# Routing stage of a mixture-of-experts kernel: low parts of weights on VectorE, token products on ScalarE, zero tiles and expert 0's weights issued later

## Chip, cores and metric

The kernel runs on one core of a Trainium2 chip. The time is that of the device for one launch, in microseconds (us). TensorE multiplies matrices into PSUM, VectorE and ScalarE work on tiles of 128 partitions in SBUF and PSUM, GpSimd does the same from SBUF and issues the gathers, and SyncE issues all other transfers. Each engine runs its own instructions in order and meets the others at semaphores.

## The reference

Sixteen sequences of attention, then a feed-forward layer with 8 experts (two chosen for each row) and one shared expert, and a residual:

```python
x = x + ffn(cond(x, mask, Wq, Wo))            # x: (16, 256, 512), so 4096 rows of 512
# ffn(x):
logits = einsum("bsh,eh->bse", x, gate_w)      # 8 experts
probs = softmax(logits); top_w, top_i = top_k(probs, 2)
top_w = top_w / sum(top_w)                     # combine: top_w at the chosen experts, else 0
h = silu(x @ w_gate[e]) * (x @ w_up[e])        # width 352, for each expert e
moe = sum over e of combine[e] * (h @ w_down[e])
shared = (silu(x @ sw_gate) * (x @ sw_up)) @ sw_down     # width 1408
return moe + shared * sigmoid(x @ shared_gate_w)
```

Everything is float32. The kernel reaches that precision with three products of rounded parts: a = hi(a) + lo(a), where hi is the value rounded to TensorE's fast format and lo is a - hi; a matmul is then hi*hi + hi*lo + lo*hi.

## The kernel before, in words

The kernel has three parts, one behind the other: `attention` (to about 735 us), `experts` (735 to about 1331 us) and `shared`. The change is in `experts` alone, and there in what comes ahead of the first expert tile: the routing stage, 735 to 837 us.

**What the routing stage computes.** It has two strands which share the engines.

- *Routing.* VectorE takes the maximum, the softmax and the two best experts of each row, in a chain of small operations each of which waits for the one before (`link`). TensorE ranks the rows by expert (`rank`, two matmuls), VectorE makes from the ranks the start of each expert's tiles (`bounds`) and the slot of each row. To invert that list, from slot to row number, there are 16 rounds of 4 blocks of rows: in a round VectorE compares (`hot_ones`: `token_at`, 128x328, is 1 where a column is the slot's column; `is_row`, 128x512, where a partition is the slot's row), GpSimd multiplies the row numbers into `token_at` (`times_token`, L798 to 802), and TensorE sums four products of the two (`place_tokens`, 4 small matmuls into `ps_id`). `token_at` and `is_row` have two buffers, so `hot_ones` of a round waits until the matmuls of the round two before are done. At the end VectorE copies the sum to `token_of`, and GpSimd gathers the rows of the first tile with it.
- *The shared expert's upward half, for the first 512 rows.* Its width of 1408 is cut into SI = 11 chunks of 128, which are the 11 steps t of TensorE's loop. A step has 12 matmuls for the gate half ("gate(t)") and 12 for the other ("up(t)"), each 128x128 by 128x512. SyncE loads a chunk's raw weights (`load_up`, 2 x 256 KB, two buffers), ScalarE makes the high part (`up_high`) and GpSimd the low part (`up_low`, L804 to 808, 128x1024), both with two buffers; ScalarE takes silu of the gate half, VectorE multiplies (`up_h`), and SyncE stores the product to `held`, to be used much later.

**The order on each engine** is written out by hand:

- TensorE, step t: wait for the chunk's low part (`a_wlo`) and silu(t-2); gate(t); the first two rounds of `place_tokens` of the step; wait for the product t-2; up(t); in step 1 `rank`; two more rounds. The rounds are in steps 6 to 9 (FIRST = 6, `rounds_after`), four each.
- ScalarE, step t: wait for gate(t), silu(t); then `up_high(t+2)`, which waits for the chunk's transfer and, as its output buffer is that of chunk t, for up(t). At the end of step 8 it makes the high parts of expert 0 (`split(0, 0)`).
- GpSimd: constants and the zero tile; `up_low(0)` to `up_low(6)`; then for t from 6 the products of two rounds, `up_low(t+1)`, the products of two more.
- VectorE: the routing chain, in which `up_h(0)` to `up_h(4)` are placed; then for t from 6 to 10 `hot_ones` of two rounds, `up_h(t-1)`, `hot_ones` of two more. After round 16 it makes `token_of`, the low parts of expert 0, the last product, and the low part of the first tile.
- SyncE's queue: the 512 rows, chunks 0 and 1, expert 0's weights (`load(0)`, 2.1 MB in four transfers), nine zero tiles into `routed` (512 KB each; slots without a row must read as zero); then in step t: wait for low part t, `load_up(t+2)`, wait for product t, store it. Behind the loop: expert 1's weights, and the wait for the zero tiles, before which no tile may be stored.

In the lists of rows a helper's line stands for all its uses: L1089 is a matmul of gate or up, L808 `up_low`, L801 `times_token`, L861 `up_high`, L872 silu, L946 `up_h`, L1025 and L1027 `hot_ones`, L1076 `place_tokens`, L739 `load_up`, L733 to L735 `load`, L748 the zero tiles, L846 and L911 the parts of an expert's weights. The buffers of the chunks' parts are those of expert 1: chunk 0, 2, ... stand as `e_hi_g` and `e_lo_g`, chunk 1, 3, ... as `e_hi_u` and `e_lo_u`; the matmuls of `place_tokens` write `e_ps_r`, and up(t) of odd steps `e_ps_y`.

Of the kernel before, what the change touches and what calls it, by code (L numbers as in the profile page):

```python
# [586 lines left out]
def experts(nc, ctx, sems, keep, attn, w_gate, w_up, w_down, sw_gate, sw_up, held, routed):  # L587
# [7 lines left out]
    P = 128  # L595
# [47 lines left out]
    RO = 4  # L643
# [74 lines left out]
        return ap.rearrange("p (a w) -> p a w", a=1).to_broadcast([P, RO, width])  # L718

    FIRST = 6  # L720

    def rounds_after(t, part):

# [5 lines left out]
    @block.sync  # L729
    def _(sp):  # L730
        def load(e):
            for k, w in enumerate((w_gate, w_up)):
                sp.dma_start(raw[k][:], w[bass.ds(e, 1), :, :].rearrange("e (k p) i -> p (e k) i", p=P)).then_inc(raw_in, 16)  # L733
            sp.dma_start(raw[2][:, 0:FULL, :], w_down[bass.ds(e, 1), 0:FULL * P, :].rearrange("e (k p) h -> p (e k) h", p=P)).then_inc(raw_in, 16)
            sp.dma_start(raw[2][0:I - FULL * P, FULL, :], w_down[bass.ds(e, 1), FULL * P:I, :].rearrange("e p h -> p (e h)")).then_inc(raw_in, 16)  # L735

        def load_up(t):
            for k, w in enumerate((sw_gate, sw_up)):
                sp.dma_start(a_raw[t % 2][:, k, :, :], w[:, t * P:(t + 1) * P].rearrange("(k p) i -> p k i", p=P)).then_inc(a_raw_in[t % 2], 16)  # L739

        sp.dma_start(a_rows[:], attn[0:GT, :].rearrange("(s p) h -> p s h", p=P)).then_inc(a_rows_in, 16)
        load_up(0)
        load_up(1)
        load(0)

        sp.wait_ge(consts, 8)
        for j in range(FEWEST, NTILES):
            sp.dma_start(routed[j * ST:(j + 1) * ST, :].rearrange("(s p) h -> p s h", p=P), zeros[:]).then_inc(filled, 16)  # L748
        for t in range(SI):
            if t + 2 < SI:  # L750

                sp.wait_ge(a_wlo, t + 1)
                load_up(t + 2)
            sp.wait_ge(a_h_done, t + 1)
            sp.dma_start(held[t * P:(t + 1) * P, :], a_h[t % 2][:]).then_inc(a_stored[t % 2], 16)
        sp.wait_ge(lo_done, NPARTS)
        load(1)
        sp.wait_ge(filled, 16 * (NTILES - FEWEST))
        sp.wait_ge(bounds_done, 1)

        def start(e, n, first):
            if exists(e + 2):

                sp.wait_ge(lo_done, NPARTS * (e + 2))
                load(e + 2)

        def tile(j, n):
            sp.wait_ge(y_done, SB * (j + 1) + SB)
            sp.dma_start(routed[bass.ds(j * ST, ST), :].rearrange("(s p) h -> p s h", p=P), y[:]).then_inc(stored, 16)

        each_expert(sp, start, tile)
        total = sp.value_load(keep["bounds"][0:1, NE:NE + 1], min_val=1, max_val=NTILES - 1)
        for n in range(2):
            sp.wait_ge(a_stored[n], 16 * ((SI - n + 1) // 2))
        keep["load_ahead"](sp)
        alone(sp, stored, 16 * total + 16, consts, 8)

    @block.gpsimd
    def _(pool):
        pool.memset(ident[:], 0.0).then_inc(base, 1)  # L780
        pool.memset(before[:], 0.0).then_inc(base, 1)
        pool.iota(iota_e[:], pattern=[[1, NE]], base=0, channel_multiplier=0, allow_small_or_imprecise_dtypes=True).then_inc(consts, 1)
        pool.wait_ge(base, 2)

        pool.affine_select(out=before[:], in_=before[:], compare_op=ALU.is_ge, fill=1.0, base=0,
                           pattern=[[-1, P]], channel_multiplier=1).then_inc(consts, 1)
        pool.memset(every[:], 1.0).then_inc(consts, 1)
        pool.affine_select(out=ident[:], in_=ident[:], compare_op=ALU.not_equal, fill=1.0, base=0,
                           pattern=[[-1, P]], channel_multiplier=1).then_inc(consts, 1)
        for tile in (iota_r, iota_c):  # L790
            pool.iota(tile[:], pattern=[[1, tile.shape[1]]], base=0, channel_multiplier=0,
                      allow_small_or_imprecise_dtypes=True).then_inc(consts, 1)
        pool.iota(token[:], pattern=[[0, TOPK], [P, NBLK]], base=0, channel_multiplier=1,
                  allow_small_or_imprecise_dtypes=True).then_inc(consts, 1)
        pool.memset(zeros[:], 0.0).then_inc(consts, 1)

        def times_token(m, n):

            pool.wait_ge(col_hot, m + 1)
            of = token[:].rearrange("p k b -> p (k b)")[:, RO * m:RO * (m + 1)]  # L800
            pool.tensor_tensor(token_at[n][:], token_at[n][:], each(of, NCOL), ALU.mult).then_inc(token_hot, 1)  # L801

        def up_low(t):
            pool.wait_ge(a_whi, t + 1)  # L804
            if t >= 2:

                pool.wait_ge(a_u_mm, t - 1)
            pool.tensor_tensor(a_lo[t % 2], a_raw[t % 2][:], a_hi[t % 2], ALU.subtract).then_inc(a_wlo, 1)  # L808

        for t in range(FIRST + 1):  # L810
            up_low(t)
        for t in range(FIRST, SI):
            for m in rounds_after(t, 0):
                times_token(m, m % 2)
            if t + 1 < SI:
                up_low(t + 1)
            for m in rounds_after(t, 1):
                times_token(m, m % 2)
        pool.wait_ge(bounds_done, 1)
        pool.wait_ge(ids_done, 1)  # L820

        def gather(j):
            pool.tensor_copy(now[:], token_of[:, bass.ds(j * SB, SB)]).then_inc(now_done, 1)
            alone(pool, now_done, j + 1, ids_done, 1)
            for s in range(SB):
                pool.indirect_dma_start(out=rows[:, s, :], out_offset=None, in_=attn,
                                        in_offset=bass.IndirectOffsetOnAxis(ap=now[:, s:s + 1], axis=0)).then_inc(rows_in, 16)

        gather(0)

        def tile(j, n):

            pool.wait_ge(rows_in, 16 * SB * (j + 1))
            pool.wait_ge(t_mm, 2 * (j + 1))
            gather(j + 1)

        each_expert(pool, lambda e, n, first: None, tile)
        total = pool.value_load(keep["bounds"][0:1, NE:NE + 1], min_val=1, max_val=NTILES - 1)
        pool.wait_ge(rows_in, 16 * SB * (total + 1))

    @block.scalar
    def _(act):
# [14 lines left out]
        def up_high(t):  # L857
# [2 lines left out]
                act.wait_ge(a_u_mm, t - 1)  # L860
            act.activation(a_hi[t % 2], a_raw[t % 2][:], ACT.Copy).then_inc(a_whi, 1)  # L861

        for m in range(HT):
            act.wait_ge(a_t_mm, m + 1)
            act.activation(a_x_hi[:, m, :], a_ps_t[m % 2], ACT.Copy).then_inc(a_xhi, 1)
        up_high(0)
        up_high(1)
        for t in range(SI):
            act.wait_ge(a_g_mm, t + 1)
            if t >= 2:  # L870
                act.wait_ge(a_h_done, t - 1)
            act.activation(a_silu[t % 2][:], a_ps_g[t % 2], ACT.Silu).then_inc(a_silu_done, 1)  # L872
            if t + 2 < SI:
                up_high(t + 2)
            if t == SI - 3:
                split(0, 0)

        act.sem_inc(y_done, SB)
# [28 lines left out]
    def _(dve):  # L907
# [28 lines left out]
        def up_x_low():  # L936
            for m in range(HT):
                dve.wait_ge(a_xhi, m + 1)
                dve.tensor_tensor(a_x_lo[:, m, :], a_ps_t[m % 2], a_x_hi[:, m, :], ALU.subtract).then_inc(a_xlo, 1)

        def up_h(t):
            dve.wait_ge(a_silu_done, t + 1)
            dve.wait_ge(a_u_mm, t + 1)
# [9 lines left out]
        link(dve.tensor_tensor(B["prob"][:], B["expd"][:], wide(R["inv"][:]), ALU.mult))  # L953

        up_x_low()
        src = "prob"
        for m, ind, one, k in (("m1", "i1", "one1", 0), ("m2", "i2", "one2", 1)):
            link(dve.reduce_max(R[m][:], B[src][:], AX.X))
# [6 lines left out]
            if k == 0:  # L965
                link(dve.tensor_scalar(B["cand"][:], B["one1"][:], -2.0, None, ALU.mult))
                link(dve.tensor_tensor(B["rest"][:], B["prob"][:], B["cand"][:], ALU.add))
                src = "rest"
                up_h(0)
        dve.tensor_tensor(B["both"][:], B["one1"][:], B["one2"][:], ALU.add).then_inc(both, 1)  # L970

        link(dve.tensor_tensor(R["ws"][:], R["m1"][:], R["m2"][:], ALU.add))
# [3 lines left out]
        link(dve.tensor_scalar(R["sgd"][:], R["sge"][:], 1.0, None, ALU.add))  # L976
        link(dve.reciprocal(keep["shared_gate"][:], R["sgd"][:]))

        up_h(1)
        dve.wait_ge(ranked, 2)  # L980
        dve.tensor_copy(B["rank"][:], ps_r[:, 0]).then_inc(copied, 1)
        dve.tensor_copy(B["count"][:], ps_r[:, 1]).then_inc(copied, 1)
# [3 lines left out]
        while d < NBLK:  # L986
            link(dve.tensor_copy(B[b][:, 0:d, :], B[a][:, 0:d, :]))
            link(dve.tensor_tensor(B[b][:, d:, :], B[a][:, d:, :], B[a][:, 0:NBLK - d, :], ALU.add))
            a, b, d = b, a, 2 * d
        up_h(2)  # L990
        link(dve.tensor_scalar(S["total"][:], B[a][:, NBLK - 1, :], 1.0 / ST, (ST - 1.0) / ST - 0.5 + 0.25 / ST, ALU.mult, ALU.add))
        link(dve.tensor_scalar(S["tiles"][:], S["total"][:], ROUND, -ROUND, ALU.add, ALU.add))
        link(dve.tensor_scalar(S["tiles"][:], S["tiles"][:], 1.0, None, ALU.max))
# [5 lines left out]
        link(dve.memset(bounds_f[:, 0:1], 0.0))  # L999
        link(dve.tensor_copy(bounds_f[:, 1:], S[c][:]))  # L1000
        dve.tensor_copy(keep["bounds"][:], bounds_f[:]).then_inc(bounds_done, 1)
        up_h(3)
        link(dve.tensor_scalar(S["start"][:], bounds_f[:, 0:NE], float(ST), None, ALU.mult))
        link(dve.tensor_tensor(B["place"][:], B[a][:], B["count"][:], ALU.subtract))
        link(dve.tensor_tensor(B["place"][:], B["place"][:], B["rank"][:], ALU.add))
# [1 line left out]
        for k, one in enumerate(("one1", "one2")):  # L1007
# [5 lines left out]
            link(dve.tensor_scalar(slot_col[:, k, :], slot_col[:, k, :], ROUND, -ROUND, ALU.add, ALU.add))  # L1013
            link(dve.tensor_scalar(slot_row[:, k, :], slot_col[:, k, :], -float(P), None, ALU.mult))
            link(dve.tensor_tensor(slot_row[:, k, :], slot_row[:, k, :], R["pf"][:], ALU.add))
            if k == 0:
                up_h(4)

        def hot_ones(m, n):

# [9 lines left out]
        for t in range(FIRST, SI):  # L1030
            for m in rounds_after(t, 0):
                hot_ones(m, m % 2)
            up_h(t - 1)
            for m in rounds_after(t, 1):
                hot_ones(m, m % 2)
            if t == FIRST + 3:
# [26 lines left out]
    def _(pe):  # L1063
# [32 lines left out]
        for t in range(SI):  # L1096
# [5 lines left out]
                pe.wait_ge(copied, 2)  # L1102
            for m in rounds_after(t, 0):
                place_tokens(m, m % 2)
            if t >= 2:
                pe.wait_ge(a_h_done, t - 1)
            up(t, 1, a_ps_u[t % 2], a_u_mm)
            if t == 1:
                rank()
            for m in rounds_after(t, 1):  # L1110
                place_tokens(m, m % 2)
        pe.wait_ge(bounds_done, 1)
# [463 lines left out]
```

## Time and profile before

| | us |
|---|---|
| median of 3 runs | 2059.78 (2058.6 to 2061.94) |
| the profiled execution | 2059.99 |
| its span | 2058.2 |
| routing stage within it | 735 to 837.06 |

| engine | busy us | share of the span |
|---|---|---|
| TensorE (PE) | 1922.2 | 93% |
| VectorE (DVE) | 1082.7 | 53% |
| ScalarE (ACT) | 709.4 | 34% |
| GpSimd (POOL) | 620.0 | 30% |

The span is the time from the first to the last instruction of the profiled execution; the measured time is a little longer. Shares are means over parts of the kernel with different limits, so what a change in one stage is worth has to be read in that stage. "PEclk" is the mean clock granted to TensorE in a stretch, as a share of full speed; its two levels are 1.2 and 2.4 GHz, 0.50 and 1.00. "SPq" is SyncE's queue of transfers. A row of a timeline begins with the start and the length of an instruction; brackets behind it give how long its engine had been idle, and what ended that.

### The profile page before, as it was taken

To read this page: it belongs to the slowest core of one execution; us is meant where nothing else is said; L and a number is where in the kernel's file an instruction comes from. 1 tells how busy PE (TensorE), PEld (TensorE's weight loads), DVE (VectorE), ACT (ScalarE), POOL (GpSimd) and SP (SyncE) were. 2 spreads that over 40 slices of the span, in tenths; PEclk is the share of its full clock that TensorE was granted. 3 is DMA by queue.
4 is the path that set the end of the run, shared out by engine and by line. 5 is a ranking of instruction groups with operands and counts; after the bars stand their busy time and mean duration, and the time that the engine had idled before them with its cause. 6 is when DMAs were issued, how large, how long until landed. Compare 5 with 4: busy or idle time off the path is not lost. (4 is left out here: it accounts for less than half of the span.)

```text
span 2058.2 us, 30150 instructions
## 1 busy us (share of the span) xinstructions
PE 1922.2 (93%) x10324; PEld 1416.7 (69%) x10325; DVE 1082.7 (53%) x1723; ACT 709.4 (34%) x1276; POOL 620.0 (30%) x444
## 2 busy tenths in 40 slices
PE   4999999999999869899999999979999999999995
PEld 2444444444444347799999999868888888888874
DVE  3788878887888548443444433343423323242334
ACT  1566666666666623232333332231010101011000
POOL 3556566666665526211111111100101001010101
PEclk6899999999999969999999999989999999999998
DMA  7776767676765063422333232162302112130204
GB/s 125 111 115 100 111 96 130 101 108 98 128 90 73 21 226 97 150 91 100 124 124 111 83 115 82 67 182 73 102 21 82 41 61 66 36 102 0 93 26 143
DMA packets 117831, 195.83 MB, mean 95 GB/s; under 512 B 11264, under 2 KB 43008, under 8 KB 117776
## 3 DMA queue, kind: packets, MB, share of 16 engines
q1 hardware_dynamic: 106736, 158.94, 34.4%
q0 software_dynamic: 11040, 36.18, 6.1%
q8 instruction: 31, 0.51, 0.1%
q14 instruction: 24, 0.20, 0.0%
HBM read 100.68 MB, written 43.25 MB: 70 GB/s over the span
## 5 line engine op out<-in xcount | busy, mean ns | idle before, releaser
L420 DVE TENSOR_REDUCE maxcol<-ps_m 128x1 f32<-128x512 f32 x512 | 336.9, 681 | 138.5 <-PE ps_m L562 133.4
L337 ACT ACTIVATE e<-ps_e 128x512 f32<-128x512 f32 x512 | 297.3, 596 | 186.5 <-PE ps_e L557 185.7
L148 POOL TENSOR_TENSOR e<-e 128x2048 f32<-128x2048 f32 x64 | 225.6, 3524 | 179.0 <-ACT e L337 178.9
L1384 DVE TENSOR_TENSOR s_h_f<-s_silu,s_ps_u 128x512 f32<-128x512 f32 x77 | 52.9, 688 | 393.5 <-PE s_ps_u L1456 344.0
L562 PE MATMUL ps_m<-kside,qside 97*128 97x512 f32 x512 | 224.3, 443 | 34.7 <-DVE maxcol L420 19.1
L1326 POOL DMA_INDIRECT s_chosen<-routed,s_slot_now x64 | 61.6, 962 | 620.9 <-DVE s_total L1430 609.6
L557 PE MATMUL ps_e<-qside,kside 98*128 98x512 f32 x512 | 236.8, 465 | 3.3 <-ACT e L337 2.1
L557 PEld LDWEIGHTS ps_e<-qside,kside 98*128 98x128 f32 x512 | 96.8, 190 | 191.8 <-ACT e L337 158.7
L1352 ACT ACTIVATE s_silu<-s_ps_g 128x512 f32<-128x512 f32 x77 | 46.0, 598 | 528.8 <-PE s_ps_g L1456 521.3
L1053 DVE TENSOR_TENSOR e_h_f<-e_silu,e_ps_h 128x256 f32<-128x256 f32 (+1 forms) x108 | 45.2, 418 | 250.1 <-ACT e_silu L894 250.1
L562 PEld LDWEIGHTS ps_m<-kside,qside 97*128 97x128 f32 x512 | 101.1, 197 | 80.6 <-DVE maxcol L420 54.6
L1467 PE MATMUL s_ps_y<-s_d_hi,s_h_hi 128*128 128x512 f32 x352 | 140.0, 398 | 10.2 <-DVE s_h_lo L1404 10.2
L1467 PE MATMUL s_ps_y<-s_d_lo,s_h_hi 128*128 128x512 f32 x352 | 138.7, 394 | 0.0
L1467 PE MATMUL s_ps_y<-s_d_hi,s_h_lo 128*128 128x512 f32 x352 | 138.7, 394 | 0.0
L455 PE MATMUL ps_num<-e,v 128*32 128x512 f32 x1024 | 138.0, 611 | 0.1
L386 DVE RECIPROCAL den<-den 128x128 f32<-128x128 f32 x128 | 119.5, 940 | 15.4 <-ACT den L268 15.4
L1456 PE MATMUL s_ps_g<-s_x_hi,s_gu_hi 128*128 128x512 f32 x308 | 121.3, 394 | 3.7 <-DVE s_d_lo L1373 3.6
L1138 PE MATMUL e_ps_h<-e_x_hi,e_hi_g 128*128 128x256 f32 (+1 forms) x432 | 122.0, 282 | 1.7 <-DVE e_x_lo L917 1.7
L1138 PE MATMUL e_ps_h<-e_x_lo,e_hi_u 128*128 128x256 f32 (+1 forms) x432 | 121.9, 282 | 0.0
L1138 PE MATMUL e_ps_h<-e_x_lo,e_hi_g 128*128 128x256 f32 (+1 forms) x432 | 121.9, 282 | 0.0
L1138 PE MATMUL e_ps_h<-e_x_hi,e_lo_g 128*128 128x256 f32 (+1 forms) x432 | 121.8, 282 | 0.0
L1138 PE MATMUL e_ps_h<-e_x_hi,e_hi_u 128*128 128x256 f32 (+1 forms) x432 | 121.6, 281 | 0.0
(233 smaller groups left out, 4189.0 us busy)
## 6 DMA issues: line engine op xcount, KB each, us to landing
routed<-e_y SPq DMA_DIRECT2D x36, 512.0 KB, 2.8
kside<-q_hi SPq DMA_DIRECT2D x64, 256.0 KB
qside<-qm_hi SPq DMA_DIRECT2D x64, 256.0 KB
x_f<-in_x SPq DMA_DIRECT2D x16, 512.0 KB, 3.5
kside<-q_lo SPq DMA_DIRECT2D x32, 256.0 KB
qside<-qm_lo SPq DMA_DIRECT2D x32, 256.0 KB
attn<-xo SPq DMA_DIRECT2D x32, 256.0 KB, 3.4
keep_rows<-attn SPq DMA_DIRECT2D x8, 1024.0 KB, 5.6
```

What stands on the lines that cost most here:

```text
L148: eng.tensor_tensor(into, into, e[k + 1][:, heads, :], ALU.add).then_inc(done, 1)
L337: act.activation(e[kb][:, g, :], ps_e[g % 2][:, :], ACT.Exp, scale=SCALE).then_inc(e_done, 1)
L386: dve.reciprocal(den[par][:, c], den[par][:, c]).then_inc(rd_done, 1)
L420: dve.reduce_max(maxcol[par][:, g * KB + kb:g * KB + kb + 1], ps_m[g % 2][:, :], AX.X).then_inc(max_done, 1)
L455: last = nc.tensor.matmul(ps_num[g * DK:(g + 1) * DK, :], v[n % RING][:, kb, g, :], e[kb][:, g, :], start=(kb == 0), stop=(kb == KB - 1))
L557: nc.tensor.matmul(ps_e[g % 2][:, :], kside[n][:, g, cols], qside[n][:, g, :], start=True, stop=True).then_inc(e_mm, 1)
L562: nc.tensor.matmul(ps_m[g % 2][:, :], qside[s2][0:MAXROW, g, cols], kside[s2][0:MAXROW, g, :], start=True, stop=True).then_inc(m_mm, 1)
L1138: last = nc.tensor.matmul(ps_h[t][0:width, k, :], l[k][:, m, at:at + width], r[:, m, :], start=(c == 0), stop=(c == len(terms) - 1))
L1326: pool.indirect_dma_start(out=chosen[k][s % 2][:], out_offset=None, in_=routed, in_offset=bass.IndirectOffsetOnAxis(ap=slot_now[:, k, s:s ...
L1384: dve.tensor_tensor(h_f[:], silu[:], ps_u[:], ALU.mult).then_inc(h_done, 1)
L1456: last = nc.tensor.matmul(ps[:], l[:, t, k, m, :], r[:, m, :], start=(c == 0), stop=(c == len(terms) - 1))
L1467: last = nc.tensor.matmul(ps_y[s][:], l[t % 2][:, c], r[:, t, :], start=(t == 0 and m == 0), stop=(t == NI - 1 and m == 2))
```

## The change

GpSimd's two tasks in the stage go to other engines, and two groups of transfers move on SyncE's queue:

- `up_low` is VectorE's. It stands at fixed places of VectorE's order: chunk 0 behind the low parts of the rows, chunk 1 in the middle of the choice of experts, chunks 2 to 6 beside `up_h`, and chunk t+1 behind `up_h(t-1)` in the loop. `up_h(0)` to `up_h(4)` come at other places of the chain than before.
- `times_token` is ScalarE's, as four activations (Copy with one scale per partition, 128x82 each) for a round: two rounds behind silu(t), two behind `up_high(t+2)`.
- `load(0)` goes to the start of SyncE's step 5, the nine zero tiles behind `load(1)`, after the loop. `split(0, 0)` on ScalarE goes from the end of step 8 to that of step 9.
- `rank` goes on TensorE from behind up(1) to between gate(1) and up(1).

```diff
@@ experts: SyncE
-        load(0)
-
-        sp.wait_ge(consts, 8)
-        for j in range(FEWEST, NTILES):
-            sp.dma_start(routed[j * ST:(j + 1) * ST, :].rearrange("(s p) h -> p s h", p=P), zeros[:]).then_inc(filled, 16)
         for t in range(SI):
+            if t == LOAD_FIRST:          # LOAD_FIRST = 5
+                load(0)
             if t + 2 < SI:
...
         load(1)
+        sp.wait_ge(consts, 8)
+        for j in range(FEWEST, NTILES):
+            sp.dma_start(routed[j * ST:(j + 1) * ST, :].rearrange("(s p) h -> p s h", p=P), zeros[:]).then_inc(filled, 16)
@@ GpSimd
-        def times_token(m, n):
-
-            pool.wait_ge(col_hot, m + 1)
-            of = token[:].rearrange("p k b -> p (k b)")[:, RO * m:RO * (m + 1)]
-            pool.tensor_tensor(token_at[n][:], token_at[n][:], each(of, NCOL), ALU.mult).then_inc(token_hot, 1)
-
-        def up_low(t):
...
-            pool.tensor_tensor(a_lo[t % 2], a_raw[t % 2][:], a_hi[t % 2], ALU.subtract).then_inc(a_wlo, 1)
-
-        for t in range(FIRST + 1):
-            up_low(t)
-        for t in range(FIRST, SI):
-            for m in rounds_after(t, 0):
-                times_token(m, m % 2)
-            if t + 1 < SI:
-                up_low(t + 1)
-            for m in rounds_after(t, 1):
-                times_token(m, m % 2)
@@ ScalarE
+        def times_token(m, n):
+
+            act.wait_ge(col_hot, m + 1)
+            of = token[:].rearrange("p k b -> p (k b)")
+            for c in range(RO):
+                last = act.activation(token_at[n][:, c, :], token_at[n][:, c, :], ACT.Copy, scale=of[:, RO * m + c:RO * m + c + 1])
+            last.then_inc(token_hot, 1)
...
             act.activation(a_silu[t % 2][:], a_ps_g[t % 2], ACT.Silu).then_inc(a_silu_done, 1)
+            for m in rounds_after(t, 0):
+                times_token(m, m % 2)
             if t + 2 < SI:
                 up_high(t + 2)
-            if t == SI - 3:
+            for m in rounds_after(t, 1):
+                times_token(m, m % 2)
+            if t == SI - 2:
                 split(0, 0)
@@ VectorE
+        def up_low(t):
+            dve.wait_ge(a_whi, t + 1)
+            if t >= 2:
+
+                dve.wait_ge(a_u_mm, t - 1)
+            dve.tensor_tensor(a_lo[t % 2], a_raw[t % 2][:], a_hi[t % 2], ALU.subtract).then_inc(a_wlo, 1)
...
         up_x_low()
+        up_low(0)
...
-                up_h(0)
+                up_low(1)
...
-        up_h(1)
+        up_h(0)
+        up_low(2)
...
-        up_h(2)
+        up_h(1)
+        up_low(3)
...
-        up_h(3)
+        up_h(2)
+        up_low(4)
...
-            if k == 0:
-                up_h(4)
+            up_h(3 + k)
+            up_low(5 + k)
...
             up_h(t - 1)
+            if t + 1 < SI:
+                up_low(t + 1)
@@ TensorE, step t
+            if t == 1:
+                rank()
             if t >= 2:
                 pe.wait_ge(a_h_done, t - 1)
             up(t, 1, a_ps_u[t % 2], a_u_mm)
-            if t == 1:
-                rank()
```

## Rows read from the trace of the kernel before

**Rows 1.** The page, engine table: busy us (share of the span) xinstructions.
```profile
PE 1922.2 (93%) x10324; PEld 1416.7 (69%) x10325; DVE 1082.7 (53%) x1723; ACT 709.4 (34%) x1276; POOL 620.0 (30%) x444
```
**Rows 2.** Stretches: us, then busy PE, PEld, DVE, ACT, POOL, PEclk, DMA, GB/s.
```profile
735.00:837.06 102.06, 79.49 (x357) 64.21 (x357) 77.54 (x126) 27.10 (x35) 51.10 (x42) 0.88 0.53 173
...
749.90:763.40 13.50, 13.43 (x49) 10.87 (x50) 9.56 (x23) 0.60 (x1) 2.44 (x1) 0.81 1.06 397
763.40:768.10 4.70, 0.97 (x5) 0.51 (x3) 1.96 (x5) 2.60 (x3) 2.34 (x2) 1.00 0.46 146
768.10:775.36 7.26, 7.20 (x24) 5.78 (x25) 5.04 (x11) 0.60 (x1) 2.39 (x2) 0.76 0.31 94
775.36:780.86 5.50, 5.50 (x26) 4.51 (x24) 4.41 (x13) 1.66 (x2) 2.42 (x1) 1.00 0.47 143
791.84:801.20 9.36, 7.78 (x41) 6.28 (x40) 9.33 (x12) 1.94 (x3) 7.30 (x6) 1.00 0.29 87
801.20:809.76 8.56, 7.62 (x42) 6.30 (x42) 7.67 (x10) 2.43 (x3) 6.82 (x6) 1.00 0.30 92
832.70:837.06 4.36, 1.10 (x8) 0.86 (x9) 2.01 (x4) 1.08 (x2) 0.77 (x2) 0.98 0.71 216
```
**Rows 3.** Waits, 735 to 842 us: total us, times, longest.
```profile
PE e_ps_h L1089 <- POOL e_lo_g L808: 8.0, 2, 4.2
...
PE e_ps_r L1076 <- POOL e_token_at L801: 4.4, 6, 0.9
```
**Rows 4.** SyncE's queue: chunk 2's gate half, expert 1's first.
```profile
753.33 1.17 SPq L739 DMA_DIRECT2D keep_raw_gu<-in_sw_gate  x1
...
833.81 0.44 SPq L733 DMA_DIRECT2D e_raw_g<-in_w_gate  x1
```
**Rows 5.** ScalarE's timeline: short rows, high parts, silu, expert 1's first part.
```profile
739.05 0.42 ACT L854 ACTIVATE e_expd<-e_shifted 128x256 f32<-128x256 f32 x1 [5.12 <-DVE e_shifted L949]
739.38 0.24 ACT L855 ACTIVATE e_sge<-keep_logits 128x32 f32<-128x32 f32 x1
...
764.63 1.06 ACT L861 ACTIVATE e_hi_g<-keep_raw_gu 128x1024 fp32r<-128x1024 f32 x1 [8.73 <-DMA keep_raw_gu<-in_sw_up]
...
775.62 1.06 ACT L861 ACTIVATE e_hi_g<-keep_raw_gu 128x1024 fp32r<-128x1024 f32 x1 [2.22 <-PE e_ps_h L1089]
...
794.79 0.60 ACT L872 ACTIVATE e_a_silu<-e_ps_h 128x512 f32<-128x512 f32 x1 [1.25 <-PE e_ps_h L1089]
...
844.44 1.38 ACT L846 ACTIVATE e_hi_g<-e_raw_g 128x1408 fp32r<-128x1408 f32 x1 [8.35 <-DMA e_raw_d<-in_w_down]
```
**Rows 6.** VectorE's timeline: like operations beside GpSimd and without.
```profile
747.54 2.57 DVE L959 TENSOR_TENSOR e_eq<-e_prob,e_m 128x256 f32<-128x256 f32 x1
...
759.20 0.43 DVE L959 TENSOR_TENSOR e_eq<-e_rest,e_m 128x256 f32<-128x256 f32 x1
...
792.01 0.50 DVE L1025 TENSOR_TENSOR e_token_at<-e_iota_c,e_slot_col 128x328 fp32r<-128x328 f32 x1
...
793.03 1.03 DVE L1025 TENSOR_TENSOR e_token_at<-e_iota_c,e_slot_col 128x328 fp32r<-128x328 f32 x1
```
**Rows 7.** VectorE's groups by form: busy us, mean ns.
```profile
L911 DVE TENSOR_TENSOR e_lo_d<-e_raw_d,e_hi_d 128x1024 fp32r<-128x1024 f32 x8 | 9.7, 1218 | 0.0
```
**Rows 8.** TensorE's timeline: step 0, then around the first rounds of step 6.
```profile
749.97 0.77 PE L1089 MATMUL e_ps_h<-e_a_x_hi,e_hi_g 128*128 128x512 f32 x1 [4.16 <-POOL e_lo_g L808]
...
794.36 0.39 PE L1089 MATMUL e_ps_h<-e_a_x_hi,e_lo_g 128*128 128x512 f32 x1
...
795.41 0.61 PE L1076 MATMUL e_ps_r<-e_token_at,e_is_row 128*128 128x82 f32 x4 [0.28 <-POOL e_token_at L801]
```
**Rows 9.** Transfers issued in 735 to 842 us: KB each, median us to landing.
```profile
keep_raw_gu<-in_sw_up SPq DMA_DIRECT2D x11, 256.0 KB, 4.1
```
**Rows 10.** ScalarE's groups by form: busy us, mean ns.
```profile
L282 ACT ACTIVATE maxrow<-ps_o 16x128 fp32r<-16x128 f32 x32 | 8.0, 251 | 6.7 <-PE ps_o L496 6.7
```
**Rows 11.** GpSimd's timeline: the products of the second round.
```profile
794.14 1.12 POOL L801 TENSOR_TENSOR e_token_at<-e_token_at,e_token 128x328 fp32r<-128x328 f32 x1 [0.43 <-DVE e_token_at L1025]
```

More of the change, by code:

```diff
@@ L720, in experts @@
     FIRST = 6
+    LOAD_FIRST = 5
     def rounds_after(t, part):
@@ L795, in _ @@
         pool.memset(zeros[:], 0.0).then_inc(consts, 1)
-        def times_token(m, n):
-            pool.wait_ge(col_hot, m + 1)
-            of = token[:].rearrange("p k b -> p (k b)")[:, RO * m:RO * (m + 1)]
-            pool.tensor_tensor(token_at[n][:], token_at[n][:], each(of, NCOL), ALU.mult).then_inc(token_hot, 1)
-        def up_low(t):
-            pool.wait_ge(a_whi, t + 1)
-            if t >= 2:
-                pool.wait_ge(a_u_mm, t - 1)
-            pool.tensor_tensor(a_lo[t % 2], a_raw[t % 2][:], a_hi[t % 2], ALU.subtract).then_inc(a_wlo, 1)
-        for t in range(FIRST + 1):
-            up_low(t)
-        for t in range(FIRST, SI):
-            for m in rounds_after(t, 0):
-                times_token(m, m % 2)
-            if t + 1 < SI:
-                up_low(t + 1)
-            for m in rounds_after(t, 1):
-                times_token(m, m % 2)
         pool.wait_ge(bounds_done, 1)
```

## The prediction

> **What bounds the kernel now.** I read the page's engine table first, then the busy time by stretch, then the waits, and last the rows of each engine around the routing stage. GpSimd is busy 30% of the span [rows 1], so it isn't the bound of the kernel; but the change touches one stage only, 735 to 837.06 us, and 102.06 us is all it can work on [rows 2]. Before it, attention is untouched; behind it, TensorE is nearly always busy.
>
> In the stage TensorE has 11 steps t, each of 24 matmuls (12 for "gate", 12 for "up"). A step without interruption takes 5.5 us (775.36 to 780.86, TensorE busy all of it). Four kinds of stretch are longer [rows 2]: steps 0 and 1 with the rank matmuls (749.97 to 764.4, half clock for the first 5 us); the stand before step 2 (4.70 us with 0.97 busy); step 2 (7.26 us at a mean granted clock of 0.76, hence 1.7 us lost); and steps 6 to 9, 9.36 us the first and 8.56 each of the others, against 5.5 plus 4 rounds of place matmuls at about 0.44 (1.75), thus 7.25. The stand before step 2 is "POOL e_lo_g", twice 8.0 us in all [rows 3], and what is behind it is a transfer: chunk 2 of the weights is issued at 753.33 behind expert 0's weights and nine zero tiles [rows 4] and ScalarE waits 8.73 us for it [rows 5]. GpSimd also costs VectorE time: one and the same operation takes 2.57 us beside a GpSimd subtraction and 0.43 without, and a token_at comparison 1.03 beside GpSimd and 0.50 without [rows 6]. In steps 6 to 9 VectorE, so slowed, is what sets 8.56.
>
> **Part by part.**
> *Low parts to VectorE.* GpSimd's 11 subtractions go, and VectorE gets 11 of 128x1024 at 1.22 us [rows 7], 13.4 us. It gets back about 2 us for each long collision (some 7 of them) and about 0.5 for each of 16 comparisons, some 22 us. Its 77.54 of 102.06 us [rows 2] fall to about 69; it isn't the bound. The first subtraction starts as before at 747.5 and ends at 748.7 instead of 749.8, so the first matmul goes from 749.97 [rows 8] to 748.8: 1.15 us gained.
> *Zeros and expert 0 later.* Chunk 2 is issued at 748.8, lands some 4.1 us later [rows 9], and is split at once when step 0 ends (756.9): high part to 758.1, low part to 760.1. Step 2 needs it at 763.05 (748.8 + 14.3 for steps 0, 1 and the rank). The stand goes, and with it the clock loss of step 2. Steps 2 to 5 then take 4 x 5.5 = 22. What is late next there is the issue of a chunk, which SyncE does behind the store of the product before; I estimate 4.1 for landing, 1.06 and 1.22 for the two parts, 1.2 to 1.5 us ahead of need in each step. Step 6 starts at 785.05, before 791.84: **6.8 us gained**.
> *The rank matmuls* move between gate and up of step 1; by my estimate "both" is ready by 757, and they come at 759.5: nothing, the same 0.9 us at another place.
> *Expert 0's load at SyncE's step 5.* It is issued at about 781.0, ahead of chunk 7 on SyncE's queue. The same load of expert 1 was issued from 833.81 and ScalarE had it at 844.44 [rows 4, 5], 10.6 us. So chunk 7 lands at 781.0 + 10.6 or a little less, 791.8 (bounds: 785.3, if it isn't held up by the load at all, to 793.3, if its own 0.5 MB comes wholly behind). ScalarE's high part of chunk 7 is waited for there, **with silu(6) and the first products queued behind it**.
> *Products on ScalarE.* Here is the main cost. The products of the first two rounds of step t are queued behind silu(t), which waits for the end of gate(t); TensorE's place matmuls stand right behind gate(t). The products of the other two are queued behind the high part of chunk t+2, which waits for the end of up(t); TensorE's place matmuls stand right behind up(t). Nothing of it is beside TensorE's work any more. Silu starts 2.95 us after the first gate matmul (gate starts at 791.84, silu at 794.79 [rows 5, 8]), ScalarE is free 0.5 later. A round is 4 activations of 128x82. No row shows one; 128x32 takes 0.24, 16x128 0.25, and rows overlap by 0.09 (128x256: 0.42 long, the next starts 0.33 on) [rows 5, 10]. Bounds: 0.15 to 0.33 start to start. I take 0.25, the nearest row's whole length, since these have a scale operand per partition besides. A round is then 1.0 us. From its end to TensorE 0.15 (GpSimd's round ended at 794.14 + 1.12 = 795.26, TensorE went on at 795.41 [rows 8, 11]), and the second round of a pair needs 0.43 more on TensorE. From gate to up: 2.95 + 0.5 + 1.0 + 0.15 + 1.0 + 0.43 = 6.0. From up to the next gate: 3.0 (chunk ready, up's end) + 0.96 + 1.0 + 0.15 + 1.0 + 0.43 = 6.55. A step is 12.55 against 8.56.
> The Trainium skill, ScalarE: Activation LUTs, "What ACT_TABLE_LOAD costs", says that a [128,1] pointer operand adds about 93 ns and that successive ACTIVATEs overlap by about as much. By that rule a round is 1.1 us and the sum stays; without the pointer's share it would be some 5 us less. No row here has a pointer operand.
> *The sum.* Step 6: chunk 7 at 791.8, high part 0.96, silu 0.5, round 1.0, 0.15, so TensorE stands from 788.0 to 794.4; up(6) starts at 795.85. After the idle 3.8 us before step 2 the granted clock fell [rows 2]; here the gap is 6.4, so up(6) runs at half clock, 12 matmuls in 5.1 instead of 2.75, and step 7 starts at 804.75 (before 801.20): +3.55. Steps 7 and 8: 2 x 4.0 = +8.0. Step 9: gate side 6.0, up 2.75, its last two rounds made beside up, placed in 0.87: 9.6 against 8.56, +1.05. That is +12.6. Then the clock: each step leaves TensorE two stretches of some 3.3 and 3.8 us with only two place rounds in them; before the experts the clock fell after 4.36 us with 1.10 busy [rows 2]. I expect it to fall in three or four of the six gaps up to step 9, 1.7 us each (step 2's loss): +5. Step 10 and the handover (832.70 to 837.06, [rows 2]) stay the same; GpSimd gathers there as before.
> *Zeros behind expert 1's load.* Nine writes of 512 KB stand on SyncE's queue behind the load, beside the first tiles' TensorE work; what queues behind them is the load for expert 2, not needed for a whole expert, and the first store of a routed tile, which comes only when a tile is done. The traffic competes with the gathers. I put it at 0 (bounds 0 to +2, if a gather is held up).
> In all 12.6 + 5 = **+17 to +18 us**. The profiled execution took 2059.99 (span 2058.2), so 2077; the median of the runs, 2059.78, is the same to 0.2 us.
>
> **Rivals.**
> A. *The serial part is cheaper.* Activations 0.15 apart (16 in a step over 3.5 steps, -5.6 us), chunk 7 not held up (-3.9), clock kept (-5 to -7 with up(6)). For it: the short rows of ScalarE do overlap. Against: all three would have to hold. It gives +2 to +10: 2062 to 2070.
> B. *The clock stays at half through steps 6 to 9.* The bursts are only 12 matmuls long. Each of the six bursts behind up(6) then costs 2.4 instead of my 5 in all: +12.6 + 14 = +27, 2086. The Trainium skill, TensorE: Matmul & The Clock Gate, "HAM oscillation", speaks for it: bursts shorter than the wait between them start cold each time. The trace is between: busy here would be 7 of 12.5 us.
> C. *Faster.* If products don't hold TensorE (ScalarE gets round to them while a half step still runs), the place rounds cost only their 1.75 and step 6 to 9 are 7.3 each: 4 x 1.3 + 6.8 = 12 less, 2048. It decides at 1.7 us of exposed delay a step; I count 5. Against it stands the order on ScalarE alone.
> D. *They cancel:* exposed delay of about 1.7 us a step, within 4 us of before.
>
> **Numbers.** Forecast (2070 to 2082) 0.55, A 0.15, B 0.17, C 0.07, D 0.06. 0.2% is 4 us, about what a measurement tells from no change. Slower 0.87, same 0.06, faster 0.07. Range 2064 to 2088: it holds the forecast, most of A, and most of B.
>
> **What would show it.** Right: no stand before step 2 and granted clock 1 in it; step 6 starting near 785; then e_ps_r waiting for ScalarE's token_at twice a step, some 1.5 to 2.5 us each, ScalarE's high part of chunk 7 waiting for a transfer, steps 7 and 8 some 12 us or more long; a lower granted clock between 790 and 835; VectorE's 2.6 us operations gone; handover and experts of the same length. Wrong: place matmuls starting without idle time (C), activations of token_at at 0.15 (A), or a stand of TensorE in steps 2 to 5, which would eat the 6.8 and make it slower yet.

## The result, and the profile after

The changed kernel takes 2083.59 us (median of 4 runs, 2079.76 to 2088.32), the kernel before 2060.39 beside it: ratio 1.0114, 95% interval [1.0091, 1.0137]. It is slower by 23 us; 2077 was forecast, between 2070 and 2082, with a range of 2064 to 2088. The profiled execution took 2082.69 us, with a span of 2080.9, 22.7 more than before.

Busy time by stretch of the kernel after; the columns are those of [rows 2]: the stage from 735.60, steps 0 to 5, then step 6, 7, 8, 9, and the handover.

```profile
735.60:859.91 124.31, 90.66 (x357) 72.25 (x357) 66.53 (x137) 43.63 (x99) 6.65 (x15) 0.81 0.34 104
749.60:786.27 36.67, 36.63 (x148) 29.89 (x149) 30.19 (x81) 9.78 (x12) 0.00 (x0) 0.92 0.43 130
786.27:805.21 18.94, 10.05 (x41) 7.93 (x40) 5.05 (x9) 6.65 (x19) 0.00 (x0) 0.82 0.47 142
805.21:818.63 13.42, 8.84 (x42) 6.99 (x42) 6.05 (x11) 5.70 (x18) 0.00 (x0) 0.94 0.19 59
818.63:835.99 17.36, 12.86 (x42) 9.93 (x42) 6.03 (x11) 5.70 (x18) 0.00 (x0) 0.70 0.15 45
835.99:849.70 13.71, 11.52 (x42) 9.17 (x42) 5.28 (x9) 7.99 (x20) 0.00 (x0) 0.70 0.05 20
...
855.50:859.91 4.41, 1.09 (x8) 0.86 (x9) 2.02 (x4) 1.08 (x2) 0.76 (x2) 1.00 0.77 229
```

Attention ends 0.59 us later than in the trace of before (its last matmuls start at 734.58, before at 733.99), so I count from there. Step 6 starts after 51.69 us, before after 57.85: **6.2 us gained**, TensorE busy for 36.63 of 36.67 us in steps 0 to 5, where it had stood 3.8 us before step 2 (8.0 - 4.2 [rows 3]). Then it goes the other way: step 7 starts 3.4 us later than before, steps 7, 8 and 9 take 13.42, 17.36 and 13.71 us instead of 8.56 each (+4.9, +8.8, +5.2), and from step 10 to the first expert matmul it is 10.21 us against 10.18. Sum: 3.4 + 4.9 + 8.8 + 5.2 = 22.3 us, which with attention's 0.6 is the whole difference of the two executions; behind the first expert matmul they are the same to 0.2 us. VectorE's busy time in the stage fell from 77.54 to 66.53 us although it has the low parts now, ScalarE's rose from 27.10 to 43.63, GpSimd's fell to 6.65.

The waits of the same stage (engine and line waited for, total us, times, longest):

```profile
POOL e_now L802 <- DVE e_token_of L1042: 111.6, 1, 111.6
...
PE e_ps_r L1080 <- ACT e_token_at L847: 20.1, 11, 6.2
...
ACT e_hi_u L840 <- DMA keep_raw_gu<-in_sw_up: 8.3, 1, 8.3
```

GpSimd waits 111.6 us for the list that its first gather needs, and does nothing in between; TensorE waits 20.1 us in all for ScalarE's products, where it had waited 4.4 for GpSimd's and 8.0 for its low parts [rows 3]. ScalarE's timeline shows the order that does it, in steps 6 and 7:

```profile
792.67 1.06 ACT L840 ACTIVATE e_hi_u<-keep_raw_gu 128x1024 fp32r<-128x1024 f32 x1 [8.35 <-DMA keep_raw_gu<-in_sw_up]
793.63 0.58 ACT L859 ACTIVATE e_a_silu<-e_ps_h 128x512 f32<-128x512 f32 x1
794.11 2.12 ACT L847 ACTIVATE e_token_at<-e_token_at,e_token 128x82 fp32r<-128x82 f32 x8
801.54 1.06 ACT L840 ACTIVATE e_hi_g<-keep_raw_gu 128x1024 fp32r<-128x1024 f32 x1 [5.31 <-PE e_ps_h L1093]
802.51 2.12 ACT L847 ACTIVATE e_token_at<-e_token_at,e_token 128x82 fp32r<-128x82 f32 x8
808.26 0.60 ACT L859 ACTIVATE e_a_silu<-e_ps_h 128x512 f32<-128x512 f32 x1 [3.63 <-PE e_ps_h L1093]
808.75 2.12 ACT L847 ACTIVATE e_token_at<-e_token_at,e_token 128x82 fp32r<-128x82 f32 x8
```

Each pair of rounds (8 activations, 2.12 us) stands behind something that waited for TensorE to end a half step (5.31, 3.63 us), or, first row, behind chunk 7, for which ScalarE waited 8.35 us. TensorE's timeline has the other half, the place matmuls and their waits:

```profile
795.37 2.06 PE L1080 MATMUL e_ps_r<-e_token_at,e_is_row 128*128 128x82 f32 x8 [6.18 <-ACT e_token_at L847]
...
803.76 0.61 PE L1080 MATMUL e_ps_r<-e_token_at,e_is_row 128*128 128x82 f32 x4 [2.31 <-ACT e_token_at L847]
...
810.01 0.61 PE L1080 MATMUL e_ps_r<-e_token_at,e_is_row 128*128 128x82 f32 x4 [1.78 <-ACT e_token_at L847]
```

It stands 6.18 us once, then 1.78 us behind every gate(t) and 2.31 behind every up(t), with 0.40 more between the two rounds in four of the seven pairs (in the other three the clock is low, and the first round's matmuls last that long). What the clock takes shows in the half steps from gate(7) to up(8), all with the same work:

```profile
805.21:811.46 6.25, 4.06 (x22) 3.15 (x22) 3.85 (x7) 2.62 (x9) 0.00 (x0) 1.00 0.42 126
811.46:818.63 7.17, 4.78 (x22) 3.84 (x22) 2.20 (x5) 3.08 (x9) 0.00 (x0) 0.88 0.00 0
818.63:827.31 8.68, 6.49 (x21) 4.86 (x22) 3.94 (x7) 2.62 (x9) 0.00 (x0) 0.70 0.30 91
827.31:835.99 8.68, 6.37 (x22) 5.08 (x22) 2.10 (x5) 3.08 (x9) 0.00 (x0) 0.70 0.00 0
```

From step 6 on the granted clock fell five times: before up(6), and before gate(8), up(8), gate(9) and up(9), four of the six gaps behind up(6). SyncE's queue: chunk 2 goes out at 749.52 (before at 753.33 [rows 4]), and chunk 7 at 784.72, behind expert 0's load.

```profile
749.52 0.37 SPq L740 DMA_DIRECT2D keep_raw_gu<-in_sw_gate  x1
...
782.24 0.43 SPq L734 DMA_DIRECT2D e_raw_g<-in_w_gate  x1
...
784.72 0.43 SPq L740 DMA_DIRECT2D keep_raw_gu<-in_sw_gate  x1
```

VectorE, the like of [rows 6]: what took 2.57 and 1.03 us beside GpSimd takes 0.42 and 0.49.

```profile
749.86 0.42 DVE L958 TENSOR_TENSOR e_eq<-e_prob,e_m 128x256 f32<-128x256 f32 x1
...
785.40 0.49 DVE L1027 TENSOR_TENSOR e_token_at<-e_iota_c,e_slot_col 128x328 fp32r<-128x328 f32 x1
```

And the row that was missing before, ScalarE's groups by form (busy us, mean ns):

```profile
L847 ACT ACTIVATE e_token_at<-e_token_at,e_token 128x82 fp32r<-128x82 f32 x64 | 17.1, 350 | 0.5 <-DVE e_token_at L1027 0.3
```

0.35 us long and, with 8 in 2.12 us, 0.253 apart. The Trainium skill, ScalarE: Activation LUTs, "What ACT_TABLE_LOAD costs", gives 186 ns + 0.833 per element, 93 more for a pointer operand and 93 of overlap. An estimate from that page is 347 ns long and 254 apart here; this case's trace agrees with 350 and 253.

### The profile page after: what moved, and what is told of

Read it like the earlier page. It is cut to its first block and busy times, and to the rows that moved or that the text cites. A ratio compares the mean times of both kernels' runs of the same rounds, so it can differ in the third digit from the quotient of the medians.

```text
span 2080.9 us, 30199 instructions
## 1 busy us (share of the span) xinstructions
PE 1932.2 (93%) x10324; PEld 1423.5 (68%) x10325; DVE 1071.9 (52%) x1734; ACT 725.8 (35%) x1340; POOL 575.8 (28%) x417
## 5 line engine op out<-in xcount | busy, mean ns | idle before, releaser
L802 POOL COPY e_now<-e_token_of 128x2 uint32 (+1 forms) x37 | 7.3, 197 | 486.2 <-PE e_ps_t L1125 374.6
```

## The experiments

Times are medians, ratios are against the kernel before on the same chip. All but e4 and e9 start from the changed kernel. Besides the medians I give the length of the stage, from attention's last matmuls to the first expert matmul, in the profiled execution: 103.1 us before, 125.3 in the kernel after. It is free of what varies outside it: attention, which no edit touches, ends between 732.93 us (e4) and 736.41 (e7) in the eleven traces.

**e1: the products back on GpSimd.**
```diff
 ScalarE:  - times_token, all calls
 GpSimd:   + for m in range(ROUNDS): times_token(m, m % 2)
```


> The changed kernel, with only the row-number products given back to GpSimd (all 16 rounds, in order, nothing else on GpSimd). Theory: the loss is the products' place in ScalarE's order, behind silu and behind the next chunk's high part, and the clock that falls in the gaps it makes. Then TensorE's waits for token_at are at most 1 us each, steps 7 to 9 take about 8.0 us (VectorE: 4 x 1.55 + 0.6 + 1.14), the clock stays at full, chunk 7's late transfer still costs step 7 about 2 us, and the time is 2052 (2049 to 2056), under that of the kernel before. Rival, that VectorE can't carry the low parts: steps 6 to 9 of 10 us or more, 2062 or above. Rival, that the moved transfers are what costs: 2075 or above.

2056.57 us, ratio 0.9983 [0.9973, 0.9992]. This one edit takes away 27 us of 2083.59, so the products' place on ScalarE is what makes the change a loss; the rivals (VectorE's load, the transfers alone) would have left 2062 or more. But it missed 2052 by 4.6. VectorE's timeline shows why:

```profile
793.84 1.22 DVE L933 TENSOR_TENSOR e_lo_u<-keep_raw_gu,e_hi_u 128x1024 fp32r<-128x1024 f32 x1 [6.48 <-ACT e_hi_u L848]
794.98 0.49 DVE L1023 TENSOR_TENSOR e_token_at<-e_iota_c,e_slot_col 128x328 fp32r<-128x328 f32 x1
```

Chunk 7 is late here too, and the wait for it now stands in VectorE's order ahead of the third comparison; I had counted it only for gate(7). So the late load does cost something here (e7 shows 8 us). TensorE's first place matmul of that pair:

```profile
796.81 1.05 PE L1076 MATMUL e_ps_r<-e_token_at,e_is_row 128*128 128x82 f32 x4 [4.30 <-POOL e_token_at L802]
```

The clock, which I had expected to stay at full, fell with that wait: step 7 takes 9.02 us at a mean of 0.80, steps 8 and 9 take 7.89 and 7.40 at 1.00. The stage is 99.6 us.

**e2: expert 0's load at the start.**
```diff
-    LOAD_FIRST = 5
+    LOAD_FIRST = 0
```


> The changed kernel, with expert 0's weights issued at SyncE's step 0 (right behind chunks 0 and 1, as before the change) and the zero tiles left at the end. Theory: chunk 7 isn't late any more, TensorE's wait in step 6 falls from 6.2 us to the 1.8 us of the other steps (-4.4), and the clock may not fall there (-1 to -2): 2078 (2075 to 2080). Nothing of the waits for ScalarE in steps 7 to 9 changes. Rival, that step 6 waits for ScalarE's work and not for a transfer: 2083. Rival, that the load at the start delays chunk 2 as before: a wait of TensorE ahead of step 2, 2083 or above.

2082.33 us (2077.02 to 2082.86), ratio 1.0102 [1.0085, 1.0119]: no gain that can be told, where 2078 was expected; the stage is 124.5 us. Yet the wait did go: TensorE's first wait in step 6 is 1.78 us instead of 6.18. The stretches of steps 6 (from 787), 7 and 8:

```profile
787.00:802.16 15.16, 10.66 (x42) 8.35 (x41) 5.50 (x10) 6.76 (x19) 0.00 (x0) 0.83 0.17 52
802.16:819.45 17.29, 12.79 (x42) 9.94 (x42) 6.06 (x11) 5.70 (x18) 0.00 (x0) 0.70 0.16 46
819.45:836.65 17.20, 12.70 (x41) 9.98 (x42) 6.05 (x11) 5.71 (x18) 0.00 (x0) 0.70 0.15 46
```

Step 7 takes 17.29 us at a mean granted clock of 0.70, against 13.42 at 0.94 in the kernel after. The 3.9 us lost there by the clock are about what step 6 won (14.9 us long instead of 18.9, counted from its first matmul at 787.25). The clock is low in all seven half steps from up(6) to up(9).

**e3: work that fills the waits.** Unread matmuls into a PSUM bank that is free in the stage.
```diff
+            if rounds_after(t, 0):
+                fill(24 if t == FIRST else 6)     # before the first pair of rounds
...
+            if rounds_after(t, 1) and t + 2 < SI:
+                fill(8)                           # before the second
```


> The changed kernel with more work on TensorE: 66 matmuls of 128x512, whose result nothing reads, ahead of the waits for the products (24 in step 6 ahead of its first pair of rounds, 6 ahead of the first pair of steps 7 to 9, 8 ahead of the second pair of steps 6 to 8); 15.1 us at 0.229 each. Theory: they fit into waits that are there anyway and keep the granted clock at full, so the low-clock stretches between 792 and 847 us go (24 us of them, of which I put down 10 to 12 us of time): 2073 (2070 to 2077). Rival, that the waits alone are the loss and the clock hardly counts: 2083 to 2086. Rival, that the added work runs into the path: above 2086.

2073.49 us (2072.68 to 2073.93), ratio 1.0067 [1.0050, 1.0083]: 66 matmuls more, and 10 us less. The granted clock is full in all of steps 7, 8 and 9:

```profile
805.30:818.37 13.07, 11.37 (x57) 8.93 (x56) 5.97 (x11) 5.71 (x18) 0.00 (x0) 1.00 0.20 60
818.37:831.43 13.06, 11.37 (x57) 8.93 (x56) 5.97 (x11) 5.71 (x18) 0.00 (x0) 1.00 0.20 60
831.43:841.33 9.90, 9.09 (x49) 7.42 (x48) 5.16 (x9) 6.55 (x19) 0.00 (x0) 1.00 0.08 28
```

So the serial part is 13.07 us a step, and what the kernel after takes beyond that is clock: its stage of 125.3 us is 115.8 here. The four runs lie within 1.3 us, those of the kernel after within 8.6, the two slower of which have a mean granted clock of 0.958 and 0.955, the two faster 0.971 and 0.972. That the fillers narrow the spread isn't shown, since the ten runs of e8, with fillers too, lie within 5.0.

**e5: all products ahead of the high part.**
```diff
             for m in rounds_after(t, 0):
                 times_token(m, m % 2)
-            if t + 2 < SI:
-                up_high(t + 2)
             for m in rounds_after(t, 1):
                 times_token(m, m % 2)
+            if t + 2 < SI:
+                up_high(t + 2)
```


> The changed kernel with two lines of ScalarE's order exchanged: all four rounds of products of a step come behind silu(t), ahead of the high part of chunk t+2. Theory: the second pair is then made beside up(t), TensorE's wait of 2.3 us behind up(t) goes in steps 6 to 8 (-2.9 each with the second round's gap), and fewer gaps bring the clock down (-3 to -6): 2071 (2067 to 2075). The wait behind gate(t) stays. Rival, that the rounds wait for VectorE's comparisons or the two buffers, whatever ScalarE's order: 2083.

2069.03 us, ratio 1.0045 [1.0029, 1.0062]: 14.6 less for two lines exchanged, as expected; the stage is 112.7 us. The waits behind up(t) are gone, six are left, and the clock fell three times instead of five:

```profile
PE e_ps_r L1080 <- ACT e_token_at L847: 12.5, 6, 6.3
```

**e4: only the zero tiles late, on the kernel before.**
```diff
-        for j in range(FEWEST, NTILES): sp.dma_start(routed..., zeros[:])    # behind load(0)
+        ... the same behind load(1)
```


> The kernel before, with one edit of the change alone: the nine zero tiles behind expert 1's load at the end of the stage (expert 0's load stays where it was, low parts and products stay on GpSimd). Theory: this is the good half of the change. Chunk 2 isn't held up any more by 4.7 MB of zeros, TensorE's wait before step 2 goes or nearly goes (-3 to -4) and the granted clock doesn't fall in step 2 (-1.7): 2055 (2054 to 2057). Rival, that the gain of 6.8 us ahead of step 6 is VectorE's, which takes the low parts and is free of GpSimd: 2060. Rival, that the zeros disturb the first expert tiles: 2060 or above.

2054.12 us, ratio 0.9972 [0.9963, 0.9982]: 6.9 us faster, as expected. No wait for a low part is left before step 2, only 0.35 us before step 4:

```profile
774.99 0.50 PE L1089 MATMUL e_ps_h<-e_a_x_hi,e_hi_g 128*128 128x512 f32 x1 [0.35 <-POOL e_lo_g L808]
```

But the stage is 100.5 us, only 2.6 shorter. Step 3 starts 5.3 us earlier than before, counted from attention; then part of it is lost, as the clock falls in steps 7 and 9, behind waits (0.35 and 0.94 us before step 7) that had left it at full in the kernel before [rows 2, 3]:

```profile
796.01:804.90 8.89, 8.89 (x42) 7.43 (x42) 5.41 (x9) 1.15 (x2) 6.64 (x5) 0.81 0.30 90
804.90:813.93 9.03, 7.71 (x42) 6.29 (x42) 8.63 (x11) 2.62 (x4) 6.94 (x6) 1.00 0.29 87
```

Of the 8.2 us between the two profiled executions, 1.1 lie in attention and 4.6 behind the stage, 2.1 of these in one wait of the first expert tile (1.77 us instead of 3.85). So the removed wait is shown, but not that all of the 6.9 us comes from it.

**e9: only the low parts on VectorE, on the kernel before** (with the places of `rank`, `up_h` and expert 0's high parts that the change has).
```diff
 GpSimd:   - up_low, all calls
 VectorE:  + up_low, as in the change
```


> The kernel before, with one edit of the change alone (beside the last): the chunks' low parts on VectorE at the places where the change has them (and the rank matmuls and products of the shared expert where the change has those); products stay on GpSimd, transfers stay as they were before the change. Theory: the two good parts of the change are separate. Zeros late alone gave -6 to -7 us (2054.1), zeros late and low parts on VectorE together -12 (2048.1); so low parts alone give -4 to -6: 2055 to 2057, as TensorE's wait before step 2 shortens only by 1.1 us (the transfer still ends it) and a step of the rounds goes from 8.56 to about 7.6. Rival, that VectorE's subtractions pay only once chunk 2 is early: 2059 to 2061.

2052.75 us, ratio 0.9955 [0.9938, 0.9971]: 8.6 us faster, more than expected. The stage is 97.0 us, 6.1 shorter. 1.5 of these are there by step 2, whose wait stays nearly as it was (3.36 us instead of 3.8; the transfer still ends it, ScalarE waits 9.47 us for chunk 2). The rest is in the steps with rounds, 7.2 to 7.9 us each instead of 8.56 and more:

```profile
766.61 0.50 PE L1089 MATMUL e_ps_h<-e_a_x_hi,e_hi_g 128*128 128x512 f32 x1 [3.36 <-DVE e_lo_g L933]
...
797.51:805.39 7.88, 7.50 (x42) 6.37 (x42) 7.49 (x12) 1.41 (x3) 4.61 (x5) 1.00 0.33 102
805.39:812.79 7.40, 7.40 (x42) 6.37 (x42) 6.55 (x10) 1.86 (x3) 4.32 (x4) 1.00 0.36 106
```

**e7: zeros late, load at the start, low parts on VectorE, products on GpSimd.** e1 with `LOAD_FIRST = 0`.

> The changed kernel with the products on GpSimd and expert 0's load at SyncE's step 0. With the load at step 5 chunk 7 is late, and VectorE stands 6.5 us at its low part with the third and fourth comparison behind it, so TensorE stood 4.3 us in step 6 and the clock fell for 6.8 us. Theory: both go with the early load (-4 and -2 to -3): 2050 (2048 to 2053). Rival, that the wait in step 6 is the chain of comparison and product: 2056, as with the late load.

2048.14 us, ratio 0.9941 [0.9924, 0.9957]: **12.8 us faster than before, 35 than the change**, 8.4 less than e1. It beats both kernels; the stage is 91.6 us, 11.5 shorter than before. TensorE is nearly never idle in the steps with rounds:

```profile
794.61:802.50 7.89, 7.55 (x43) 6.40 (x42) 7.46 (x12) 1.23 (x3) 4.61 (x5) 1.00 0.33 102
802.50:809.90 7.40, 7.40 (x42) 6.36 (x42) 6.56 (x10) 1.91 (x3) 4.31 (x4) 1.00 0.36 106
```

e4 and e9 gave 6.9 and 8.6, 15.5 in sum, and together it is 12.8; but with intervals of 2 us and more on each that is no clear difference, and by the stage it goes the other way (2.6 + 6.1 = 8.7 against 11.5).

**e8: e3 with the load at the start.**
```diff
-                fill(24 if t == FIRST else 6)
+                fill(6)
-    LOAD_FIRST = 5
+    LOAD_FIRST = 0
```


> The changed kernel with expert 0's load at SyncE's step 0 and the unread matmuls that fill TensorE's waits (6 ahead of the first pair of every step 6 to 9, 8 ahead of the second pair of steps 6 to 8, 48 in all). With the early load alone TensorE's wait in step 6 went from 6.2 to 1.8 us and yet the time stayed: the clock fell seven times instead of five. Theory: the 4.4 us were taken back by the clock; with the clock held at full they show: 2069 (2067 to 2071), 4.4 less than the fillers with the late load (2073.5). Rival, that the early load costs 4 us somewhere else: 2073 or above.

2065.70 us, ratio 1.0023 [1.0013, 1.0032], 7.8 less than e3, where 4.4 less was expected. With the clock held, the early load shows its gain, which it didn't in e2 (there are 18 matmuls fewer ahead of the first pair, which the shorter wait has no room for). The stage itself is 110.5 us against 115.8 in e3, so most of the gain is in it. Another 1.8 us of the two profiled executions lie in attention, which the edit doesn't touch (its last matmuls in e3, then in e8):

```profile
735.83 1.02 PE L521 MATMUL ps_o<-add_up,partial 128*128 128x9 f32 x4 [0.50 <-ACT partial L321]
...
734.03 1.02 PE L521 MATMUL ps_o<-add_up,partial 128*128 128x9 f32 x4 [0.50 <-ACT partial L321]
```

**e6: place matmuls half a step later.**
```diff
-    FIRST = 6
+    FIRST = 5
-            for m in rounds_after(t, 0): place_tokens(m, m % 2)       # behind gate(t)
+            for m in rounds_after(t - 1, 1): place_tokens(m, m % 2)
-            for m in rounds_after(t, 1): place_tokens(m, m % 2)       # behind up(t)
+            for m in rounds_after(t, 0): place_tokens(m, m % 2)
```
(with `LOAD_FIRST = 0`, and `up_h(4)` and `up_low(6)` in VectorE's loop.)

> A version meant to beat both: the changed kernel (products on ScalarE, low parts on VectorE, zeros late) with expert 0's load at step 0, the rounds in steps 5 to 8 instead of 6 to 9, and TensorE's place matmuls half a step later than the products' place in ScalarE's order: first pair behind up(t), second behind gate(t+1). Theory: what cost time is only that TensorE stood right behind what ScalarE waits for; with half a step between, products and comparisons are made beside matmuls, a step is 5.5 + 4 x 0.44 = 7.25 us, the clock stays at full, and the gather of tile 0 is done before step 10 ends: 2046 (2044 to 2050). Rival, that four rounds of products don't fit on ScalarE beside high parts and silu (4 x 1.0 + 1.0 + 0.5 = 5.5 of 7.25 us) or that VectorE's order holds them up: 2055 or above.

2059.52 us, ratio 0.9993 [0.9984, 1.0003]: 24 less than the change, but no gain over before and far from 2046; the rival with VectorE's order came true, and my reason was short by a link. ScalarE's timeline:

```profile
797.31 1.06 ACT L840 ACTIVATE e_hi_g<-keep_raw_gu 128x1024 fp32r<-128x1024 f32 x1 [4.38 <-DMA keep_raw_gu<-in_sw_up]
798.27 2.12 ACT L847 ACTIVATE e_token_at<-e_token_at,e_token 128x82 fp32r<-128x82 f32 x8
```

The second pair still stands behind the high part, and in each of steps 6 to 8 that waits 4.4 us for its transfer: SyncE issues chunk t+2 behind the store of product t-1, VectorE makes that product behind comparisons, and these wait for place matmuls that now come later. The circle closes through four engines; the three high parts start 10.0 us apart. The stage is still 98.2 us, 4.9 shorter than before, which the median doesn't show: 1.9 of it go in the first expert tile, where TensorE waits 5.76 us instead of 3.85, and the rest I can't place.

## Why the prediction was right, point by point

- *The early gain.* 6.8 forecast, 6.2 measured; e4 and e9 show its two sources apart: by step 6 the one has gained 4.7 us, the other 1.5. VectorE's relief was as sized (77.54 to 66.53 us; 69 forecast).
- *Chunk 7 behind expert 0's load.* Issue to ScalarE 10.6 forecast, 10.4 measured (782.24 to 792.67); TensorE's wait 6.2 against 6.4. Step 7 started 3.42 us late against 3.55. What I didn't see is that VectorE's order holds comparisons behind it as well (e1).
- *The products in ScalarE's order.* The mechanism was right, and e1 and e5 show it. A step at full clock is 13.07 us (e3), forecast 12.55: a round's last activation is 0.35 long and not 0.25, twice a step (0.2), and the rest of the 0.5 is spread over the handovers. In all, with the clock at full (e3), the stage is 115.83 - 103.07 = 12.8 us longer; my serial terms, without the half clock of up(6), were 10.2. So this term was 2.6 too small, 0.9 of it in step 6 and 1.0 in steps 7 and 8.
- *The clock.* This term was mis-sized too, by 2.1. I put down 5 us and 2.35 in up(6), 7.4; the kernel after has 22.3 - 12.8 = 9.5. The number of falls was right: behind up(6) the forecast was three or four, and there were four. But a fall costs some 2.1 us there and not 1.7: step 8, with two of them, takes 17.36 - 13.07 = 4.3 us more than at full clock. Rival B, low all through, would have made +27; the trace lies between.
- *The number.* The two terms erred the same way, so the result is 6.6 us above 2077 and outside 2070 to 2082. It is inside the range because that was drawn to hold most of rival B, to whose 2086 the measured 2083.6 is nearer.
- *Zeros at the end, handover.* 0 forecast, 10.21 against 10.18 us measured.
- *Rivals.* A needed activations 0.15 us apart, and they are 0.253. C and D needed products beside TensorE's work; all but the last pair stood behind it, and e5 shows what that cost: with the second pair made beside up(t) the kernel is 14.6 us faster.

Open: why attention ends up to 3.5 us apart in traces of the same code, and why the granted clock fell five times in the profiled execution of the kernel after, seven times in that of e2, and twice in that of e4, where waits are shorter than 1 us.

## What to carry to other kernels

An engine that is idle otherwise can be the right place for a job, because the job then waits for nothing but its inputs: 16 products of 1.1 us cost 27 us on ScalarE, where each takes about as long as on GpSimd, because there they stand behind waits for the very engine that needs them. Before moving a job, write down what is ahead of it in the new engine's order and what that waits for; if it is the consumer's last work, the job is serial. And read short waits of TensorE with the granted clock beside them: a wait removed can come back as clock (e2), and matmuls nobody reads can save time (e3).

## What was not expected of the hardware

- Waits of only 1.78 and 2.31 us between bursts of 12 matmuls were enough to bring the granted clock down, but not each time: 0.94 in step 7 and 0.70 in step 8, with the same waits. In e4 it fell twice behind waits of less than 1 us, which had left it at 1.00 before. Filled to 0.4 to 0.5 us (e3) they kept it at 1.00.
- A late transfer reached TensorE through each engine that waited for it in order: 8.35 us on ScalarE in the kernel after, 6.48 on VectorE, behind ScalarE, in e1.
- Parts that an edit doesn't touch vary by as much as a small gain: attention ended between 732.93 and 736.41 us in eleven traces. A gain of 2 or 3 us is better read in its stage than in medians of a few runs.
